# An attention and mixture-of-experts block: weights laid out transposed in memory, the second matrix loaded behind the attention

## The reference

```python
xh = x.reshape(8, 512, 16, 8)
xc = xh - mean(xh, axis=1, keepdims=True)
corr = softmax(einsum('bthd,bThd->bhtT', xc, xc), axis=-1)
x = layernorm(x + einsum('bhtT,bThd->bthd', corr, xh).reshape(8, 512, 128))
# 4096 tokens; topk_idx and topk_w from sigmoid(x @ gate_weight.T), sorted by expert
xe = zeros((64, 128, 128)).at[sorted_e, pos].set(tok_sorted, mode='drop')
h = silu(einsum('ech,efh->ecf', xe, w1)) * einsum('ech,efh->ecf', xe, w3)
ye = einsum('ecf,ehf->ech', h, w2)
out = segment_sum(where(pos < 128, ye[sorted_e, pos], 0) * flat_w, flat_t, 4096)
shared = silu(x @ shared_gate.T) * (x @ shared_up.T) @ shared_down.T
x = layernorm(x + out + shared)
```

## Time and profile before

| | us |
|---|---|
| median of 3 runs (739.41, 743.42, 743.62) | 743.42 |
| the profiled execution, as timed | 746.63 |
| its span, first to last instruction | 744.9 |
| PE busy in the span (mean granted clock 0.80) | 422.9 |
| ACT busy | 387.0 |
| POOL busy | 386.4 |
| DVE busy | 340.0 |

### The profile page before, as it was taken

One profiled execution on the slowest core, in us unless ns is written; L12 is line 12 of the kernel. 1 busy time (PEld: TensorE's weight loads), 2 busy tenths in 40 slices (PEclk: granted clock), 3 DMA queues, 4 the chain that ended last, 5 costly groups with the idle time before them and its releaser, 6 DMA issues.

```text
span 744.9 us, 9051 instructions
## 1 busy us (share of the span) xinstructions
PE 422.9 (57%) x2932; PEld 194.9 (26%) x2932; DVE 340.0 (46%) x1102; ACT 387.0 (52%) x516; POOL 386.4 (52%) x431
## 2 busy tenths in 40 slices
PE   4888989828757863881677587435200655655000
PEld 4223333312222321230222122214200644543000
DVE  5316776724825743580456147286300524342156
ACT  2798999818656863891586596312200422220026
POOL 2000035626643662645366266665666288888846
PEclk9799999969977996996798899856755876675555
DMA  3999931100000000000000000000000765533398
GB/s 99 217 266 241 189 81 38 31 1 10 20 5 7 4 17 4 3 18 2 2 3 18 1 4 17 2 16 3 1 2 1 196 100 79 79 36 35 36 233 226
DMA packets 83125, 43.66 MB, mean 59 GB/s; under 512 B 13319, under 2 KB 82707, under 8 KB 83072
## 3 DMA queue, kind: packets, MB, share of 16 engines
q1 hardware_dynamic: 61568, 36.18, 20.3%
q0 software_dynamic: 21504, 6.81, 8.0%
HBM read 21.27 MB, written 44.40 MB: 88 GB/s over the span
## 4 chain that ended last, share of the span: by engine, by line
PE 27%; POOL 22%; issue 21%; ACT 18%; DVE 5%; DMA 3%; SPq 1%; another core or an unknown queue 1%; POOLq 0%; ACTq 0%; DVEq 0%
ACT large L911 14%; POOL sums L532 12%; POOL records L509 9%; PE S L663 9%; PE PV L677 8%; PE M L583 2%; PE M L576 2%; ACT OT L896 2%; PE PV L687 2%; SPq L435 1%; DMA records<-rec,index 1%; DMA sums<-centred,target 1%; DMA large<-sums 1%; PE M L612 1%
## 5 line engine op out<-in xcount | busy, mean ns | idle before, releaser
L509 POOL DMA_INDIRECT records<-rec,index x256 | 254.6, 995 | 162.8 <-issue 83.8
L911 ACT ACTIVATE large<-S,shift_now 128x1024 f32<-128x1024 f32 x256 | 277.7, 1121 | 77.1 <-PE S L663 67.9
L663 PE MATMUL S<-LR 64*128 64x512 bf16 x512 | 103.9, 409 | 105.5 <-DVE LR L1162 64.0
L677 PE MATMUL PV<-large,V 128*9 128x512 f32 x1024 | 141.4, 626 | 0.2 <-ACT large L911 0.2
L532 POOL DMA_INDIRECT sums<-centred,target x64 | 99.1, 1548 | 35.4 <-issue 18.9
L663 PEld LDWEIGHTS S<-LR 64*128 64x128 bf16 x512 | 24.3, 93 | 251.2 <-ACT large L911 129.8
L488 POOL PARTITION_ALL_REDUCE largest_all<-largest x8 | 3.0, 372 | 99.4 <-DMA records<-blank 39.6
L980 ACT COPY AK<-S 128x512 f32<-128x512 f32 x16 | 9.3, 584 | 70.0 <-PE S L790 70.0
L1162 DVE COPY LR<-M 128x1024 bf16<-128x1024 bf16 x42 | 28.8, 685 | 36.1 <-PE M L583 34.4
L790 PE MATMUL S<-ident,X 128*128 128x128 f32 x64 | 14.5, 371 | 49.7 <-DMA X<-records 49.7
L687 PE MATMUL PV<-ident,OT 128*128 128x128 f32 x128 | 21.0, 287 | 23.3 <-ACT OT L896 19.9
(11 more groups left out here) (180 smaller groups left out, 792.4 us busy)
## 6 DMA issues: line engine op xcount, KB each, us to landing
records<-blank SPq DMA_DIRECT2D x1, 6176.0 KB, 30.3
X<-records SPq DMA_DIRECT2D x16, 386.0 KB, 3.7
large<-sums SPq DMA_DIRECT2D x24, 256.0 KB, 4.9
sums<-blank SPq DMA_DIRECT2D x2, 2112.0 KB
large<-L_ffn_w_dram SPq DMA_DIRECT2D x2, 2048.0 KB, 21.2
records<-rec,index POOLq DMA_INDIRECT x256
X<-L_attn_x_dram SPq DMA_DIRECT2D x8, 256.0 KB, 2.8
sums<-Z SPq DMA_DIRECT2D x8, 256.0 KB
```

The lines of the kernel that those rows point to most:

```text
L509: pool.indirect_dma_start(records, bass.IndirectOffsetOnAxis(ap=index[:, i * TOP + k:i * TOP + k + 1], axis=0), rec[:, i, :], None, bounds ...
L663: mm = pe.matmul(S[:, 2 * (n % 2) + j, :], LR[rows, pair, 0, tile * P:(tile + 1) * P], LR[rows, pair, 1, :], start=True, stop=True)
L677: mm = pe.matmul(PV[g % 2][32 * i:32 * i + VCOLS, :], V[:, 2 * c + k, QUAD * g + i, :], E[:, u % 2, i, k, :], start=c == 0 and k == 0, sto ...
L911: nc.scalar.activation(E[:, u % 2, 2 * (i // 2):2 * (i // 2) + 2, i % 2, :], S[:, 2 * (n % 2):2 * (n % 2) + 2, :], ACT.Exp, bias=shift_now ...
```

## The change

The weights are laid out before the launch: w1 and w3 joined and transposed to (h, expert, f of w1 and f of w3), w2 to (a * 64 + f, pair of experts, h), where a says which expert of the pair, and gate and shared matrices transposed. The small matrices are loaded into `small_T` directly, and w13 in one transfer where three transfers of weights were. PE's turning of small and expert weights, and the copies behind it, are gone. w2 is loaded by SP in two halves, straight to the diagonal blocks of `w2bd`, when the last attention matmul has read `E` (`unit_weighed`); this wait stands ahead of the last batch's `sums<-Z`. DVE clears only the blocks beside the diagonal, in two memsets. PE waits once for all of that ahead of the experts' loop.

```diff
-                    sp.dma_start(small_w[0:EXPERTS, 0, :], gate_w).then_inc(small_loaded, 16)
-                    sp.dma_start(small_w[:, 1, :], s_gate).then_inc(small_loaded, 16)
+                    sp.dma_start(small_T[:, 0, 0:EXPERTS], gate_w).then_inc(small_loaded, 16)
+                    sp.dma_start(small_T[:, 1, :], s_gate).then_inc(small_loaded, 16)
...
-            sp.dma_start(w13[0:FF, :, :], w1.rearrange("e f h -> f e h")).then_inc(weights_loaded, 16)
-            sp.dma_start(w13[FF:P, :, :], w3.rearrange("e f h -> f e h")).then_inc(weights_loaded, 16)
-            sp.dma_start(w2n[:, :, :], w2.rearrange("e h f -> h e f")).then_inc(weights_loaded, 16)
+            sp.dma_start(w13, w13_in).then_inc(weights_loaded, 16)
 
             for q in range(BATCHES):
+                if q == BATCHES - 1:
+                    sp.wait_ge(unit_weighed, UNITS * BATCHES)
+                    for a in range(2):
+                        sp.dma_start(w2bd[a * FF:(a + 1) * FF, :, a * DIM:(a + 1) * DIM],
+                                     w2_in[a * FF:(a + 1) * FF, :, :]).then_inc(w2_loaded, 16)
...
-            for k in range(4):
-                rows = EXPERTS if k == 0 else P
-                mm = pe.transpose(PV[1][:, k * P:k * P + rows], small_w[0:rows, k, :], ident[0:rows, 0:rows])
-            mm.then_inc(small_turned, 1)
             for o in range(2):
                 pe.wait_ge(first_taken[o], 4)
-            pe.wait_ge(small_ready, 5)
             iterations(pe, batch)
...
-            pe.wait_ge(weights_loaded, 16 * 3)
-            for n in range(WEIGHT_JOBS):
-                bank = n % 2
-                pe.wait_ge(read[bank], epilogue_end[bank] + n // 2)
-                for i in range(4):
...
-                    mm = pe.transpose(M[bank][:, i * P:(i + 1) * P], src, ident[:, :])
-                mm.then_inc(written[bank], 1)
...
+            pe.wait_ge(weights_loaded, 16)
+            pe.wait_ge(w2_loaded, 16 * 2)
+            pe.wait_ge(w2_cleared, 2)
...
-            v.tensor_copy(small_T[:, 0, 0:EXPERTS], PV[1][:, 0:EXPERTS]).then_inc(small_ready, 1)
-            v.tensor_copy(small_T[:, 1:4, :], PV[1][:, P:4 * P].rearrange("p (a c) -> p a c", a=3)).then_inc(small_ready, 1)
             dve.wait_ge(small_loaded, 16 * 5)
-            dve.wait_ge(small_ready, 5)
+            dve.wait_ge(small_ready, 3)
             iterations(dve, batch)
...
-            v.memset(w2bd, 0.0).then_inc(w2_cleared, 1)
-            dve.wait_ge(w2_cleared, 1)
-            for n in range(0, WEIGHT_JOBS, 2):
...
+            for a in range(2):
+                v.memset(w2bd[a * FF:(a + 1) * FF, :, (1 - a) * DIM:(2 - a) * DIM], 0.0).then_inc(w2_cleared, 1)
```

More of the change, by code:

```diff
@@ L81, with post_norm_block @@
 SCALE_STEPS = ["minus_mean", "veps", "r2", "vr2", "corr", "rstd", "offset"]
-def post_norm_block(nc, x, gate_w, e_bias, w1, w2, w3, s_gate, s_up, s_down, out):
+def post_norm_block(nc, x, gate_w, e_bias, w13_in, w2_in, s_gate, s_up, s_down, out):
     with ExitStack() as ctx:
@@ L112, in post_norm_block @@
         bias = sb("bias", [P, EXPERTS])
-        small_w = sb("small_w", [P, 4, P])
         small_T = sb("small_T", [P, 4, P])
@@ L237, in post_norm_block @@
         small_loaded = sem("small_loaded")
-        small_turned = sem("small_turned")
         small_ready = sem("small_ready")
@@ L266, in post_norm_block @@
         w2_cleared = sem("w2_cleared")
+        w2_loaded = sem("w2_loaded")
         slots_loaded = [sem(f"slots_loaded{j}") for j in range(4)]
@@ L390, in _ @@
                 if q == 0:
-                    sp.dma_start(small_w[0:EXPERTS, 0, :], gate_w).then_inc(small_loaded, 16)
-                    sp.dma_start(small_w[:, 1, :], s_gate).then_inc(small_loaded, 16)
-                    sp.dma_start(small_w[:, 2, :], s_up).then_inc(small_loaded, 16)
-                    sp.dma_start(small_w[:, 3, :], s_down).then_inc(small_loaded, 16)
+                    sp.dma_start(small_T[:, 0, 0:EXPERTS], gate_w).then_inc(small_loaded, 16)
+                    sp.dma_start(small_T[:, 1, :], s_gate).then_inc(small_loaded, 16)
+                    sp.dma_start(small_T[:, 2, :], s_up).then_inc(small_loaded, 16)
+                    sp.dma_start(small_T[:, 3, :], s_down).then_inc(small_loaded, 16)
                     sp.dma_start(bias[:, :], e_bias.rearrange("(a e) -> a e", a=1).to_broadcast([P, EXPERTS])
@@ L819, in _ @@
             w2bd_flat = w2bd.rearrange("p r c -> p (r c)")
+            pe.wait_ge(weights_loaded, 16)
+            pe.wait_ge(w2_loaded, 16 * 2)
+            pe.wait_ge(w2_cleared, 2)
             for o in range(2):
-                pe.wait_ge(read[o], epilogue_end[o] + WEIGHT_JOBS // 2)
+                pe.wait_ge(read[o], epilogue_end[o])
             pe.wait_ge(pv_read, QUADS * BATCHES)
@@ L961, in _ @@
             gate_sigmoid(BATCHES - 1)
[L964 to L974, removed]
             def copy_x(s, u):
@@ L1402, in _ @@
             post_totals("epilogue", BATCHES, p)
-            v.memset(w2bd, 0.0).then_inc(w2_cleared, 1)
-            dve.wait_ge(w2_cleared, 1)
-            for n in range(0, WEIGHT_JOBS, 2):
[L1406 to L1410, removed]
-                    r = 4 * (n - EXPERTS // 4)
-                    v.tensor_copy(w2bd[0:FF, r:r + 4, 0:DIM], src[0:FF, :, :])
-                    v.tensor_copy(w2bd[FF:P, r:r + 4, DIM:2 * DIM], src[FF:P, :, :]).then_inc(read[0], 1)
+            for a in range(2):
+                v.memset(w2bd[a * FF:(a + 1) * FF, :, (1 - a) * DIM:(2 - a) * DIM], 0.0).then_inc(w2_cleared, 1)
             def add_one(s, u):
@@ L1503 @@
     from concourse.bass_utils import run_bass_kernel_spmd
+    w1, w2, w3 = (inputs[f"L0_ffn_w{k}"] for k in (1, 2, 3))
+    laid_out = {
+        "attn_x": inputs["L0_attn_x"],
+        "gate_weight": inputs["L0_ffn_gate_weight"].T,
+        "e_bias": inputs["L0_ffn_e_bias"],
+        "w13": np.concatenate([np.transpose(w1, (2, 0, 1)), np.transpose(w3, (2, 0, 1))], axis=2),
+        "w2": np.transpose(np.reshape(w2, (EXPERTS // 2, 2, DIM, FF)), (1, 3, 0, 2)).reshape(P, EXPERTS // 2, DIM),
+        "shared_gate": inputs["L0_ffn_shared_gate"].T,
+        "shared_up": inputs["L0_ffn_shared_up"].T,
+        "shared_down": inputs["L0_ffn_shared_down"].T}
     nc = bacc.Bacc("TRN2", target_bir_lowering=False, num_devices=1)
     arrays, args = {}, []
-    for name in _INS:
-        a = np.ascontiguousarray(inputs[name])
+    for name, a in laid_out.items():
+        a = np.ascontiguousarray(a)
         arrays[f"{name}_dram"] = a
```

5 lines of the change are left out of this document (removed).

## The result

The changed kernel takes 750.64 us (median of 8 runs, 747.07 to 753.25), the kernel before 743.52 us in the same comparison (8 runs). The ratio is 1.0095, 95% interval 1.0064 to 1.0125: 7.1 us slower, under the 1% that was to count as a difference. Its profiled execution took 753.25 us, with a span of 751.5.

The account below looks back on a forecast made before the run. PE and ACT were taken to bound the kernel to 100 us, then POOL. Terms -0.4 + 0 + 0 + 5.0 - 0.6 = +4.0 on the 743.42 us median gave 747.4 us, range 739.8 to 756.2.

Parts of the forecast that it names:

- The case that carried this forecast: w2's load beside the record scatters after the attention: a passing delay of 1.5 to 7.3 us, chance 0.55.
- the starved rival: POOL's landing waits end only as w2's load drains, 472 to 485 us: +12.8 - 1.0, 755 us; chance 0.19.
- What bounds the kernel: PE and ACT set the pace from 20 to 100 us, then POOL; the weights' turning lies beside this.
- Weight jobs: Dropping 24 weight jobs (96 transposes and copies) before the experts is worth 0, since POOL's scatters cover them.
- the program's term: Some 250 fewer instructions, about one program-load packet, from POOL's stretch after 500 us: -0.6 us, bounds 0 and 2.4.
- Small weights: At the start, small weights not turned: first score matmul at 19.80 instead of 20.19 us, gain 0.4 us.
- w13: w1 and w3 in one early transfer, landed before 90 us; attention beside it no faster: worth 0.
- The rival of held-up program loads: w13's long runs in the early load hold up program fetches: +3 us, 750.4 us in all; no separate chance.
- w2 beside the scatters: w2's load after the attention delays landings that POOL's scatters wait for: +5.0 us, bounds 0 and 12.8.
- the scaling from the stores sums<-Z: Excess POOL idle time beside 256 KB stores, 0.51 us each, scaled by bytes to w2's load: 4.1 to 5.9 us.
- The check by "0.9 us late each": Seven landing waits during w2's load in two interleaved chains, 3.5 steps, each about 0.9 us late: 3.2 us.
- The round-robin rule: DMA engines drain a whole packet before switching queues; beside w2's load 0.4 to 0.8 us per landing, 1.5 to 2.8 in all.

Follow-up runs that it names:

- e5: The kernel before with four landing semaphores for each record buffer instead of two, for all batches; ratio 1.0084 to the kernel before.
- e2_no_w2_load: The changed kernel without any load of w2 (SP's one wait and two transfers dropped); ratio 0.9960 to the kernel before.
- e8_pieces: The changed kernel with w2 loaded at the same place in 16 pieces of 128 KB, each awaited before the next; ratio 1.0057 to the kernel before.
- e3_rows_apart: The changed kernel with w2 laid out so the same 2 MB load moves rows of 512 bytes lying 64 KB apart; ratio 1.0081 to the kernel before.
- e12: The changed kernel with a second 2 MB load, to LR, queued right behind w2's; ratio 1.0185 to the kernel before.
- e1_w2_early: The changed kernel with w2 loaded at the start into its own buffer and copied to w2bd by ACT; ratio 0.9960 to the kernel before.
- e9: e1_w2_early with four landing semaphores for the last two batches' scatters alone; 731.93 us, ratio 0.9833 to the kernel before.
- e10: The kernel before with four landing semaphores for the last two batches' scatters alone; 732.29 us, ratio 0.9828.

## Why the prediction came out as it did

The measured time lies in the range, and "within 1%" was the likeliest of the three. That it came out so was in part luck. The case that carried this forecast, a delay of 1.5 to 7.3 us, did not occur: the load cost 10.1 us, beyond the 8.4 us from which I had said that the starved rival decides. The total stayed at +7.1 us because the rest of the change gained 3.0 us (uncertain by 2.2) and not the 1.0 that I took; with 1.0 it would have been +9.1, slower by my own line of 7.4. Point by point:

- **What bounds the kernel.** Right where the change touches it: the turning was not on the path. That POOL alone makes the pace of the attention is not borne out: in e5 its scatters hardly wait for a landing any more, and the cycle did not fall, since they wait for exponentials instead. The change took 100 matmuls and their copies from PE, ACT and DVE; e2_no_w2_load, which has nothing but that and the small layout gains, is 0.4% faster.
- **Weight jobs: 0.** Right for their own time (PE idle 77.91 instead of 49.73 us). The side effect on POOL, which I had in the program's term, was 1.5 us where I took 0.6, inside my bound of 2.4.
- **Small weights: -0.4.** Measured -0.34 at the first score and -0.28 at the first scatter.
- **w13: 0.** 43.61 against 43.57 us for batch 1; w13 landed 13.8 us after its issue, by 76 us, where I had said before 90. Right. The rival of held-up program loads did not show.
- **w2 beside the scatters: +5.0.** The mechanism (POOL waits for landings that the load delays) and the place were right; the size was half of what came. The term measured 9.3 us in the two traces (8.72 plus the 0.57 that after was ahead) and 10.1 us between the ratios. Of the signs, the DMA share near 1 for 12 us was there, at 466 to 478 instead of 472 to 485 us. The excess idle time was 9.2 us where 4 to 6 was named, the longest stretch 7.07 us, nearer to the 10 of the starved rival. The last scatter minus the end of the attention grew from 103.0 to 117.0 us, by 14 and not by 4; 6.7 of these 14 are only the earlier end of the attention, so that sign was a poor one. The step that failed is the scaling from the stores sums<-Z: 0.51 us for each 256 KB, 4.1 to 5.9 for 2 MB. A store of 1 us is over well within the 2.9 us that a scatter may take to land unnoticed, while the load of 12 us outlasts it. So the stores show what a brush with a load costs, and not what a long load costs. The upper figure, 5.9, also rested on the idle time of 2.15 us at 504.37, which is not the store's: it stands at batch 6's 17th scatter, and e8_pieces has 3.10 us there (503.81) with the last store only at 519.69. And w2 was taken to have the stores' form, runs of 512 bytes, where its packets were 7.3 KB; e3_rows_apart shows that this made no difference to the wait. The check by "0.9 us late each" repeated the same fault. The loads of 1, 2 and 4 MB show 5.3, 10.1 and 16.8 us. A nearer number was to be had from before: had POOL got out only what it may issue without a landing, two scatters, the loss would be the load's 12 us less 2 x 1.46 us, 9 us. It is right for 2 MB alone: for 1 MB it gives 3 us and for 4 MB 19, where the waits show 5.8 and 17.2. That is the rival "starved", to which I gave 0.19 and a price of 12.8 less 1.0. It came nearer than the forecast's case, but not to the letter: landings do come while the load moves, some 10 us late (e12).
- **The round-robin rule.** From the Trainium skill, "DMA: Bandwidth & Descriptors", section "Queues, rings and completion order", I estimated 0.4 to 0.8 us for each landing with typical packets, 3 us at the most. The traces show landings of 9 to 12 us beside a load of 12, with rows of 512 bytes as with packets of 7.3 KB. The measurement decides: the estimate from that rule was far too low. Which stage of a scatter waits (its rows, its data or its signal) stays open. In after, POOL's queue moved nothing between 466 and 471 us, then 41 packets until 472, 5 to 6 us behind the issue of the scatter at 465.71, and POOL had its landing 3 to 4 us behind these.
- **The total.** +4.0 was forecast, +7.1 measured. Of that w2's load is +10.1 where I took 5.0, and the rest of the change -3.0 (ratio 0.9960, with 2.2 us of uncertainty on either side) where I took -1.0; the stages hold 0.3 and 1.5 us of those 3.

## What to carry to other kernels

A transfer that "has slack" still costs what it delays on the DMA engines: look for small transfers in whose landing another engine waits, and take the long transfer's duration, less what that engine may issue without a landing, as a first estimate of the loss (9 us here for 2 MB, where 9.2 to 10.1 were measured; too low for 1 MB, too high for 4). A short overlap in the trace is no measure for a long one. The load belonged where no one waits for a landing, in the first 100 us (e1_w2_early); and more transfers in flight paid only where no attention ran beside them (e9 and e10 against e5).

## What the runs showed of the hardware

- A record scatter, 48 packets and some 3 KB moved, landed 9 to 12 us after issue beside a 2 MB load, whatever the load's packet size (7.3 KB or 512 bytes), and 9 to 11 us after issue in the midst of a load of 4 MB. Alone it lands within the 2.9 us in which POOL, two in flight, comes to the scatter two behind it.
- With four scatters in flight POOL issues one each 1.28 us instead of 1.46. In the three kernels with four in flight during the attention, ACT and PE stood still there for some 6 us at a time; what released them stays open.
- Batch 6's stage of scatters repeats between kernels to 0.05 us (46.83 to 46.86 us in the five without turning and without a load there), so its length told apart what ratios with intervals of 0.6% could not. Batch 5's, which runs beside the end of the attention, does not (46.02 to 50.24).
